# A two-layer decoder on one core: the last batch of the last FFN by halves, and the instruction lists in another order

## The reference

```python
def act_quant(x):                       # per token
    scale = 128 / clip(max(abs(x), axis=-1), 1e-5)
    return clip(round(x * scale), -128, 127) / scale
def bitlinear(x, w):   return act_quant(x) @ weight_quant(w).T
def h_bitlinear(x, w): return act_quant(fwht(x)) @ weight_quant(w).T
# FFN: h = silu(bitlinear(x, w_gate)) * bitlinear(x, w_up)      256 -> 1024 features
#      out = h_bitlinear(h, w_down)                             1024 -> 256
# y = layernorm(x + out), written out
```

## Time and profile before

| | us |
|---|---|
| median of 3 runs (lowest, highest) | 695.84 (695.28, 696.39) |
| the profiled execution: its own time | 695.4 |
| the profiled execution: span from the first to the last instruction | 693.3 |
| TensorE busy in the span | 668.4 (96%) |
| VectorE, GpSimd, ScalarE busy | 605.5, 570.5, 423.5 |

### The profile page before, as it was taken

The page is one execution under the profiler, slowest core; times in us unless marked ns, Lnnn a source line. Parts: engine busy times, 40 slices in busy tenths (PEclk is TensorE's granted clock), DMA queues, the critical chain, the costliest instruction groups (busy, mean ns, idle before and its releaser), DMA issues. The chain is left out here.

```text
span 693.3 us, 13904 instructions
## 1 busy us (share of the span) xinstructions
PE 668.4 (96%) x4318; PEld 482.1 (70%) x4318; DVE 605.5 (87%) x1329; ACT 423.5 (61%) x692; POOL 570.5 (82%) x750
## 2 busy tenths in 40 slices
PE   8999999999999899998899999999999999999994
PEld 7888888754444577786688888855444477777883
DVE  5988889679999998878899999889999998888774
ACT  1765666721370686976798888830101468888985
POOL 3986988987878699994467889999988989989952
PEclk9999999999999999999999999999999999999998
DMA  8820000000400050000211111122000000000001
GB/s 309 334 107 1 2 2 2 2 1 0 182 0 0 1 213 21 2 2 1 95 62 61 61 62 62 62 75 66 0 0 1 0 1 2 16 17 17 16 17 45
DMA packets 12726, 33.39 MB, mean 48 GB/s; under 512 B 2672, under 2 KB 8048, under 8 KB 11376
## 3 DMA queue, kind: packets, MB, share of 16 engines
q1 hardware_dynamic: 12080, 31.99, 12.5%
q10 hardware_dynamic: 576, 0.53, 0.3%
HBM read 30.35 MB, written 2.16 MB: 47 GB/s over the span
## 5 line engine op out<-in xcount | busy, mean ns | idle before, releaser
L1084 PE MATMUL bank<-XT,win_late 128*128 128x256 f32 x320 | 79.8, 385 | 2.0 <-DVE ss_xc L1269 1.6
L632 DVE TENSOR_REDUCE MIX<-m_pr 128x128 f32<-128x1024 f32 x64 | 76.6, 1206 | 0.4
L1269 DVE SCALAR_TENSOR_TENSOR ss_xc<-bank,cw_late,ss_xc 128x254 f32<-128x254 f32 x144 | 67.7, 477 | 6.2 <-ACT ss_xc L1173 2.7
L577 POOL TENSOR_TENSOR m_kv<-CTXT 128x512 f32<-128x512 f32 x64 | 65.1, 1042 | 7.4 <-PE bank L609 7.2
L577 POOL TENSOR_TENSOR m_kv<-XT,CTXT 128x512 f32<-128x512 f32 x64 | 68.0, 1089 | 1.4 <-PE bank L609 1.4
L607 PE MATMUL bank<-m_kv,toep 128*128 128x512 f32 x128 | 66.3, 600 | 1.2 <-POOL m_kv L577 1.0
L609 PE MATMUL bank<-m_kv,toep 128*128 128x512 f32 x128 | 65.4, 592 | 0.0
L608 PE MATMUL bank<-m_kv,toep 128*128 128x512 f32 x128 | 65.4, 592 | 0.0
L1084 PEld LDWEIGHTS bank<-XT,win_late 128*128 128x128 f32 x320 | 56.7, 190 | 11.9 <-DVE ss_xc L1269 4.3
L1562 PE MATMUL bank<-had_last,f_ht 128*128 128x256 f32 x256 | 59.4, 379 | 0.0
L445 POOL TENSOR_TENSOR at_p<-at_p,at_mx 128x512 f32<-128x512 f32 x44 | 45.0, 1041 | 10.6 <-DVE at_mx L355 10.5
(11 more groups left out here) (255 smaller groups left out, 1946.6 us busy)
## 6 DMA issues: line engine op xcount, KB each, us to landing
MIX<-cum_rows SPq DMA_DIRECT2D x15, 512.0 KB, 3.6
toep<-toep_dram SPq DMA_DIRECT2D x2, 2048.0 KB, 12.3
X<-x_dram SPq DMA_DIRECT2D x1, 2048.0 KB, 13.8
CTXT<-ctxT_dram SPq DMA_DIRECT2D x1, 2048.0 KB, 17.5
out_dram<-f_o SPq DMA_DIRECT2D x16, 128.0 KB, 1.7
XT<-xT_dram SPq DMA_DIRECT2D x1, 1280.0 KB, 9.3
win_late<-win_dram SPq DMA_DIRECT2D x1, 1280.0 KB, 5.2
wgu<-wgu_dram SPq DMA_DIRECT2D x1, 1024.0 KB, 5.2
```

Source lines behind the costliest of these rows:

```text
L577: m = nc.gpsimd.tensor_tensor(KV[n % 3][:, c, :, :].rearrange("p (b j) i -> p b j i", b=HB), ki, vj, ALU.mult)
L632: nc.vector.tensor_reduce(head(MIX)[:, :, a, bass.ts(h, HB), :], PR[n % 2][:, :, :, :].rearrange("p c (b j) i -> p c b j i", b=HB), op=ALU ...
L1084: m = nc.tensor.matmul(bX[(NU * g + n) % 3][:, 0:GS_], win[:, h, off:off + P], XT[:, h, bass.ts(g, GS_)], start=(h == 0), stop=(h == C - 1))
L1269: m = nc.vector.scalar_tensor_tensor(acc[:, :, sh:S], bank[:, :, 0:S - sh], cw[:, r, n:n + 1], acc[:, :, sh:S], ALU.mult, ALU.add)
```

## The change

For batches 0 to 14 every call stays as it is. For batch 15, V is not copied: the two keep_v(15, k) calls are gone from ScalarE's list. v_peak(15) reduces each half where it stands in PSUM and then the two results (its two half reductions now signal what the copies signalled). whole(15), drop(15), w_turn(15), keep_w(15) and the product down(15) each go by two halves of 512 features; the second half of the turned blocks goes to another PSUM bank, b3.

```diff
+    bQT, bWT, bWT_end = (bank[:, :].bitcast(BF16) for bank in (bQ, bW, b3))
 # w_turn
+            if n == B - 1:
+                for k, bank in enumerate((bWT, bWT_end)):
+                    pe.wait_ge(s["w_made"], B + k)
+                    for r in range(4 * k, 4 * k + 4):
+                        m = nc.tensor.transpose(bank[:, bass.ts(r, S)], W[:, bass.ts(r, P)], identb[:, :])
+                    m.then_inc(s["w_turned"], 1)
+                return
 # down
+                if n == B - 1 and r == FC // 2:
+                    pe.wait_ge(s["w_kept"], B + 1)
 # keep_v
-            if not 0 <= n < B:
+            if not 0 <= n < B - 1:
 # whole
+            if n == B - 1:
+                for k in range(2):
+                    nc.scalar.activation(R[:, bass.ts(k, 512)], bV[k][:, :], ACT.Identity, scale=SH[n % 4][:, :],
+                                         bias=rnd[:, :]).then_inc(s["rounded"], 1)
+                return
 # keep_w
+            if n == B - 1:
+                for k, bank in enumerate((bWT, bWT_end)):
+                    act.wait_ge(s["w_turned"], B + k)
+                    nc.scalar.copy(WT[:, 4 * k:4 * k + 4, :], bank[:, bass.ts(k, 512)].rearrange("p (r s) -> p r s", r=4)).then_inc(s["w_kept"], 1)
+                return
 # v_peak
+            if n == B - 1:
+                for k in range(2):
+                    dve.wait_ge(s[f"v{k}_made"], B)
+                    nc.vector.tensor_reduce(peaks[:, k:k + 1], bV[k][:, :], op=ALU.max, axis=AX.X,
+                                            apply_absolute_value=True).then_inc(s[f"v{k}_kept"], 1)
             dve.wait_ge(s["v0_kept"], n + 1)
             dve.wait_ge(s["v1_kept"], n + 1)
+            if n == B - 1:
+                nc.vector.tensor_reduce(HM_[n % 4][:, :], peaks[:, :], op=ALU.max, axis=AX.X).then_inc(s["v_peaks"], 1)
+                return
 # drop
+            if n == B - 1:
+                for k in range(2):
+                    dve.wait_ge(s["rounded"], B + k)
+                    half = bass.ts(k, 512)
+                    nc.vector.tensor_scalar(W[:, half], R[:, half], ROUND + 127.0, ROUND, ALU.min, ALU.subtract).then_inc(s["w_made"], 1)
+                return
```

All four lists are also written in another order, from the first stage to the last. Apart from the two keep_v calls they hold the same calls as before: 919 on TensorE (409 at the same place, none more than 12 places away), 1066 on VectorE, 463 on POOL, 663 instead of 665 on ScalarE. The places that the prediction speaks of:

```diff
 # tensor, last batches
- h_turn(15,0) w_turn(13) h_turn(15,1) down(12) transform(15,0) transform(15,1) down(13) w_turn(14) down(14) w_turn(15) down(15)
+ h_turn(15,0) h_turn(15,1) w_turn(13) down(12) transform(15,0) transform(15,1) down(13) w_turn(14) down(14) w_turn(15) down(15)
 # scalar, last batches
- keep_v(14,1) keep_h(15,0) keep_v(14,0) keep_h(15,1) norm_out(10) keep_w(13) whole(14) keep_v(15,0) keep_v(15,1) norm_out(11)
+ keep_v(14,1) norm_out(10) keep_h(15,0) keep_v(14,0) keep_h(15,1) keep_w(13) whole(14) norm_out(11)
 # (both go on: keep_w(14) whole(15) norm_out(12) keep_w(15) norm_out(13) norm_out(14) norm_out(15))
 # vector, last batches
- v_peak(14) add_down(12) v_step(14) v_scale(14) stats3(12) drop(14) aggregate3(12) v_peak(15) v_step(15) v_scale(15) add_down(13) drop(15) stats3(13) add_down(14) aggregate3(13)
+ v_peak(14) add_down(12) v_step(14) v_scale(14) drop(14) v_peak(15) v_step(15) stats3(12) aggregate3(12) v_scale(15) add_down(13) stats3(13) aggregate3(13) drop(15) add_down(14)
 # tensor, start of the last FFN
- mix(24) mix_turn(3) skip(3) mix(25) mix(26) mix(27) mix_turn(4) skip(4) q_turn(0) mix(28) q_turn(1) gate(0,1) up(0,1) gate(0,0) up(0,0)
+ mix_turn(3) mix(24) skip(3) q_turn(0) mix(25) mix(26) mix(27) up(0,1) gate(0,1) mix(28) gate(0,0) mix_turn(4) up(0,0) q_turn(1) skip(4)
 # vector, start of the last FFN
- stats(2) aggregate(1) times_q(23) aggregate(2) step_size(0) times_q(24) skip_times(3) scale(0)
+ stats(2) aggregate(1) step_size(0) scale(0) aggregate(2) times_q(23) times_q(24) skip_times(3)
 # scalar, start of the last FFN
- norm_x(0) norm_x(1) lift(0) norm_x(2) lift(1) quantise(0)
+ norm_x(0) lift(0) quantise(0) norm_x(1) lift(1) quantise(1)
```

More of the change, by code:

```diff
@@ L1856, in tensor_order @@
[L1856 to L1859, removed]
@@ new lines, in vector_order @@
+    g.add_mix(7); g.stats(7); g.drop(0); g.multiply(3, 0); g.keep_q(5); g.aggregate(7); g.multiply(3, 1); g.peak(6); g.v_peak(1); g.step_size(6)
+    g.peak(7); g.v_step(1); g.scale(6); g.add_down(0); g.v_scale(1); g.multiply(4, 0); g.drop(1); n.add_up(31); g.multiply(4, 1); g.stats3(0)
+    g.v_peak(2); g.v_step(2); g.keep_q(6); g.v_scale(2); g.step_size(7); g.skip_times(8); g.scale(7); g.skip_add(8); g.add_mix(8); g.stats(8)
+    g.drop(2); g.aggregate(8); g.multiply(5, 1); g.multiply(5, 0); g.aggregate3(0); g.add_down(1); g.peak(8); g.step_size(8); g.v_peak(3); g.v_step(3)
@@ new lines, in vector_order @@
+    g.stats3(1); g.v_scale(3); g.skip_times(9); g.aggregate3(1); g.skip_add(9); g.add_mix(9); g.scale(8); g.multiply(6, 0); g.multiply(6, 1)
+    g.keep_q(7); g.drop(3); g.add_down(2); g.stats3(2); g.stats(9); g.v_peak(4); g.v_step(4); g.aggregate(9); g.aggregate3(2); g.skip_times(10)
+    g.skip_add(10); g.v_scale(4); g.keep_q(8); g.add_mix(10); g.drop(4); g.peak(9); g.stats(10); g.step_size(9); g.scale(9); g.multiply(7, 0)
+    g.multiply(7, 1); g.add_down(3); g.stats3(3); g.aggregate(10); g.skip_times(11); g.skip_add(11); g.add_mix(11); g.v_peak(5); g.peak(10)
@@ new lines, in vector_order @@
+    g.step_size(10); g.stats(11); g.keep_q(9); g.v_step(5); g.scale(10); g.v_scale(5); g.aggregate(11); g.multiply(8, 0); g.aggregate3(3)
+    g.add_down(4); g.drop(5); g.multiply(8, 1); g.v_peak(6); g.skip_times(12); g.v_step(6); g.v_scale(6); g.skip_add(12); g.add_mix(12); g.stats(12)
+    g.peak(11); g.step_size(11); g.scale(11); g.stats3(4); g.keep_q(10); g.drop(6); g.aggregate(12); g.add_down(5); g.aggregate3(4); g.multiply(9, 0)
+    g.multiply(9, 1); g.v_peak(7); g.peak(12); g.skip_times(13); g.skip_add(13); g.add_mix(13); g.stats3(5); g.v_step(7); g.keep_q(11)
@@ new lines, in vector_order @@
+    g.step_size(12); g.v_scale(7); g.scale(12); g.stats(13); g.multiply(10, 0); g.aggregate(13); g.multiply(10, 1); g.drop(7); g.add_down(6)
+    g.v_peak(8); g.peak(13); g.skip_times(14); g.step_size(13); g.scale(13); g.v_step(8); g.skip_add(14); g.aggregate3(5); g.v_scale(8); g.add_mix(14)
+    g.keep_q(12); g.stats(14); g.stats3(6); g.aggregate(14); g.multiply(11, 0); g.drop(8); g.add_down(7); g.multiply(11, 1); g.v_peak(9); g.keep_q(13)
+    g.peak(14); g.skip_times(15); g.v_step(9); g.v_scale(9); g.skip_add(15); g.step_size(14); g.scale(14); g.aggregate3(6); g.add_mix(15); g.stats(15)
@@ new lines, in vector_order @@
+    g.multiply(12, 1); g.aggregate(15); g.multiply(12, 0); g.stats3(7); g.drop(9); g.v_peak(10); g.add_down(8); g.keep_q(14); g.v_step(10)
+    g.v_scale(10); g.stats3(8); g.peak(15); g.step_size(15); g.scale(15); g.drop(10); g.aggregate3(7); g.multiply(13, 0); g.multiply(13, 1)
+    g.aggregate3(8); g.v_peak(11); g.v_step(11); g.add_down(9); g.v_scale(11); g.keep_q(15); g.multiply(14, 1); g.multiply(14, 0); g.drop(11)
+    g.v_peak(12); g.v_step(12); g.stats3(9); g.v_scale(12); g.add_down(10); g.multiply(15, 1); g.aggregate3(9); g.multiply(15, 0); g.drop(12)
```

609 lines of the change are left out of this document (296 added, 313 removed).

## The result

| | before | after |
|---|---|---|
| median, us (lowest, highest) | 695.56 (694.70, 696.39), 4 runs | 716.38 (716.25, 716.49), 4 runs |
| ratio, 95% interval | | 1.0298 (1.0282 to 1.0313) |
| profiled execution, span | 695.4, 693.3 | 716.25, 714.5 |

The account below looks back on a forecast made before the run. TensorE was taken as the bound, busy 668.4 of 693.3 us. The profiled 695.4 less 0.7 for the tail and 0 for the lists gave 694.7, or 695.1 by the median; range 692.9 to 697.9.

Parts of the forecast that it names:

- What bounds it: Whole kernel: TensorE busy 668.4 of 693.3 us, with 14.8 us of idle time spread over the body before the tail.
- Parts one to four, the tail: Batch 15: V left in PSUM, two half peaks, then scaling to down product by halves; gain 0.7 us, 0.3 to 1.3.
- The half peak out of PSUM: v_peak(15) on VectorE: each 128x512 reduction takes 0.68 us, the first starting after drop(14).
- the gain of the peak had no buyer: Peak 0.6 us earlier, but whole(15) cannot start before 681.5, behind keep_w(14); both parts together worth minus 0.2.
- The half activation: whole(15) on ScalarE: each 512-column activation out of PSUM takes 0.695 us, bounds 0.48 and 0.81.
- Part five, the lists: All other calls reordered on the engines: effect 0, plus or minus 1.7 us, on TensorE's 14.8 us of body idle time.
- a wait above 1.1 as a sign of being wrong: TensorE at q_turn(0) or anywhere in the body: a wait above 1.1 us would show the forecast wrong.
- Rival (c): Lists open a new wait, such as 2.7 us at the last FFN's q_turn(0); plus 2.0, 697.8 us; chance 0.20.
- (a): The tail gives its full paper sum, 2.9 us: copy, peak and overlapped halves; 692.9 us; chance 0.05.
- (b): The lists also close waits in the body, by 0.8 to 3 us, say 1.8; 693.3 us; chance 0.30.
- (d): The halves do nothing, since VectorE's queue ahead of drop holds everything; 695.8 us; chance 0.45 together with the forecast.

Follow-up runs that it names:

- tail_only: The changed code of batch 15 with the four lists of before, less the two keep_v(15, k) calls; 694.57 us, ratio to before 0.9990.
- new_ssm: The changed code with the lists of before, except the new order on all four engines in the state space; 701.03 us, ratio to before 1.0082.
- ffn0_weights: The changed code, new order in FFN 0 only, with m.ternary(0) and m.to_whole(2) put back ahead of keep_q(0); 696.12 us, ratio to before 1.0009.
- lists_only: The code of before with the four new lists, keep_v(15, 0) and keep_v(15, 1) behind whole(14); 719.08 us, ratio to before 1.0345.

## Why the prediction was wrong

**What bounds it** was right: TensorE, with 14.8 us of idle time in the body, which only the lists' order could change.

**Parts one to four, the tail**, held in the changed kernel, within 0.3 us. The half peak out of PSUM took 0.68 (I took 0.68), and both began right behind drop(14). keep_w(14) ended 0.09 behind the reciprocal and held whole(15), so the gain of the peak had no buyer; I had put it 0.2 ahead of the reciprocal, and so whole(15) started 2.31 behind the last transform, not 2.6. The half activation took 0.77 (0.695, within 0.48 to 0.81). aggregate3(13) ended at drop's start. down(15) came 6.30 us behind the last transform (about 6.5). The tail's gain was 0.87 in the two profiled executions (I said 0.7). The 0.7 of tail_only's runs is no second proof: there the path is another one, with the old order of VectorE, and that the size agrees is partly luck. Two halves of keep_w(15) took 1.07 against 1.01 for the whole one, about the 0.07 that I had read from copies in a row; the estimate of 1.14 by the Trainium skill (VectorE: DVE Perf Modes, section The TRN2 errata — SBUF-src ops pay a fixed extra latency per instruction) did not come about, nor its 0.06 more for a reduction out of PSUM (0.682 against 0.676).

**Part five, the lists**, is the step that failed. It said 0, "plus or minus 1.7", "about an eighth of the idle time either way", and "this part can only move the 14.8 us of idle time". Measured: 21.8 us (716.38 less 694.57), more than the idle time that I let it play with. TensorE's idle time in the body is 32.1, and it waits 2.55 us in FFN 0, where I had named a wait above 1.1 as a sign of being wrong. Two errors are in it. First, 14.8 us is a bound only for what an order can gain; what it can lose has no such bound, for work that was hidden comes out from behind TensorE. Second, I took calls that move few places for a small change. m.ternary(0) and m.to_whole(2) are some 2 us long, and in the old list they stand where ScalarE has nothing to do, ahead of keep_q(0); in the new one they stand between calls that TensorE waits for. That could be read beforehand from two lists and one duration. It explains 4.6 of FFN 0's 6.1 us with the other stretches old; with all lists new, taking it away gave 1.9 by the medians. I had looked only at the two ends of the lists' diff that the code change touched, and at one start of a stage.

**Rival (c)** had the right sign and mechanism in kind, a wait that the lists open, but not the place and not the size: at q_turn(0) of the last FFN TensorE does not wait. Its chance of 0.20 and price of 2.0 were both too small, since 510 calls in another place on TensorE alone (919 less 409) got one mechanism. **Rivals (a), (b) and (d)** did not happen.

**What stays open.** In attention, the state space and the last FFN (4.5, 6.3 and 5.6 us by the traces) no single call is the cause that I could show, and 1.5 us of FFN 0 are open too. What else the traces add is in the last section; it was read, not tested.

## What to carry to other kernels

When four engines' lists are written in another order, price them by the long calls: list each call over 1 us on an engine that feeds the bound one, and see what stood behind it before and stands behind it now. A bound engine's idle time limits the gain of an order and not its loss, so without a full replay the range must be lopsided. And lists come as a set: change the code under proven lists first (here 0.7 us, and about 0.6 more from one move that one wait pointed at), then test an order stretch by stretch.

## What the hardware showed

**VectorE and GpSimd.** In new_ssm, one VectorE instruction (L1301, both inputs in SBUF) took 2.40 us; in most other places it takes about 0.68.

```profile
433.35 1.90 POOL L1375 TENSOR_TENSOR MIX<-CUM,MIX 128x1024 f32<-128x1024 f32 x1
433.39 2.40 DVE L1301 TENSOR_TENSOR ss_y<-ss_ysum,ss_sz 128x512 f32<-128x512 f32 x1
```

It started 0.04 us behind a 1.90 us product of GpSimd and ended 0.55 us behind that one's end. This is so wherever this instruction took over 1 us, three times in tail_only (1.32, 1.13, 1.02) and three times in new_ssm (1.44, 2.40, 1.55): each time it started while a GpSimd tensor_tensor of over 1 us was running, and ended 0.54 to 0.55 us behind its end. All the other runs show the same. As I read it, the VectorE instruction stood still until GpSimd's was through. In the other order it is GpSimd's that gets longer: at 362.5 us in tail_only L1375 started 0.07 us behind L1301, which took its 0.69, and L1375 took 2.37 instead of 1.90. The new order only makes VectorE meet longer ones; over the 16 of a kernel, tail_only and then new_ssm:

```profile
L1301 DVE TENSOR_TENSOR ss_y<-ss_ysum,ss_sz 128x512 f32<-128x512 f32 x16 | 13.1, 817 | 0.2
```

```profile
L1301 DVE TENSOR_TENSOR ss_y<-ss_ysum,ss_sz 128x512 f32<-128x512 f32 x16 | 14.5, 906 | 0.3
```

The Trainium skill (GPSIMD Engine Reference, section Key points) says that GpSimd shares its SBUF interfaces with VectorE, with contention for VectorE instructions that have two SBUF inputs. These traces agree, with 1.7 us in the worst case. An order of calls thus changes durations too, not only waits; in this line it is 1.4 us of VectorE's time, and what of it reaches the 6.3 us of the state space is not shown.

**The clock behind one wait.** In the changed kernel TensorE was busy for 3.17 of the 5 us from 250 us on, at a granted clock of 1.00, and then waited 2.55 us; the next two windows of 5 us have 0.70 and 0.96. Where the wait was 0.8 us, in ffn0_weights, the clock stayed at 1.00. In the tail of lists_only it fell behind a wait of 2.19 us. These are readings; no run changed a wait alone.
